# Attention and mixture-of-experts layer, one core: the first two chunks' work in another order, decay matrix and up-weight copy split

## The reference

```
weights = exp(tanh(((xn @ W + b) @ xn.T) * decay))      # decay[s,t] = 1/|s-t|, 0 on the diagonal
weights = weights * (1 - eye);  weights /= sum + 1e-7;  attn = weights @ xn
scores  = sigmoid(xn @ gate_w.T); top 2 of 8 experts by scores + expert_bias
h       = relu(up_e(score * xn))**2 in bf16; routed = sum over the two experts of down_e(h)   # hidden size 176
shared  = relu(xn @ shared_up.T)**2 @ shared_down.T
out     = x + attn + routed + shared
```

## Time and profile before

| | |
|---|---|
| median of 3 runs | 126.49 us |
| profiled execution, whole | 126.78 us |
| its span, first to last instruction | 125.0 us |
| PE busy | 113.0 us (90%) |
| DVE busy | 100.3 us (80%) |
| ACT busy | 90.5 us (72%) |
| POOL busy | 69.3 us (55%) |
| granted TensorE clock | 1.00 (2.4 GHz) throughout |

### The profile page before, as it was taken

The page is one execution under the profiler, slowest core; times in us unless marked ns, Lnnn a source line. Parts: engine busy times, 40 slices in busy tenths (PEclk is TensorE's granted clock), DMA queues, the critical chain, the costliest instruction groups (busy, mean ns, idle before and its releaser), DMA issues.

```text
span 125.0 us, 2786 instructions
## 1 busy us (share of the span) xinstructions
PE 113.0 (90%) x915; PEld 84.6 (68%) x915; DVE 100.3 (80%) x312; ACT 90.5 (72%) x133; POOL 69.3 (55%) x122
## 2 busy tenths in 40 slices
PE   2978874797999999999999999999999999999691
PEld 2964354375767877687958695878588767778491
DVE  5794794996888898898899889889888688988721
ACT  1215859697858977897969796988689768996730
POOL 4329827997499139943896369716981514141000
DMA  3999000699365993968394939487778656868952
GB/s 97 366 394 359 16 0 0 127 144 127 69 122 112 97 226 60 171 124 152 67 208 81 167 74 188 81 192 90 148 85 199 123 106 125 199 115 48 238 149 84
DMA packets 47821, 17.28 MB, mean 138 GB/s; under 512 B 44992, under 2 KB 45760, under 8 KB 47808
## 3 DMA queue, kind: packets, MB, share of 16 engines
q1 hardware_dynamic: 47232, 15.44, 63.3%
q10 hardware_dynamic: 576, 1.68, 3.8%
HBM read 3.84 MB, written 2.10 MB: 47 GB/s over the span
## 4 chain that ended last, share of the span: by engine, by line
PE 76%; POOL 8%; ACT 4%; DMA 4%; DVE 3%; issue 2%; POOLq 0%; DVEq 0%; ACTq 0%
PE out_ps L768 13%; PE h_ps L737 13%; PE side L714 10%; PE dots L697 9%; PE out_ps L756 5%; PE side L726 5%; PE out_ps L797 4%; PE small L689 4%; DMA hiddenT<-hidden 4%; PE out_ps L750 4%; PE small L674 3%; PE small L666 3%; POOL xn L242 3%; DVE gated L542 1%; PE small L683 1%
## 5 line engine op out<-in xcount | busy, mean ns | idle before, releaser
L542 DVE SCALAR_TENSOR_TENSOR gated<-h_ps,gates 128x1408 bf16<-128x1408 f32 x31 | 50.0, 1614 | 6.9 <-PE h_ps L737 5.9
L412 ACT ACTIVATE hidden<-gated 128x1408 bf16<-128x1408 bf16 x31 | 42.6, 1379 | 3.7 <-DVE gated L542 3.4
L768 PEld LDWEIGHTS out_ps<-downT,hiddenT 128*128 128x128 bf16 x341 | 21.6, 98 | 7.6 <-issue 3.4
L737 PE MATMUL h_ps<-upT,xnTb 128*128 128x512 bf16 (+1 forms) x96 | 24.4, 362 | 1.2 <-DVE gated L542 0.9
L768 PE MATMUL out_ps<-downT,hiddenT 128*128 128x128 bf16 x341 | 24.1, 219 | 1.2 <-DMA hiddenT<-hidden 1.2
L242 POOL TENSOR_SCALAR xn<-x_sb,meanvar,rstd 128x128 f32<-128x128 f32 x28 | 22.0, 796 | 0.7
L267 POOL TENSOR_SCALAR_AFFINE_SELECT probs<-probs 128x256 f32<-128x256 f32 x16 | 6.5, 408 | 23.5 <-ACT probs L378 23.5
L714 PE MATMUL side<-xn,probs 128*128 128x129 f32 x128 | 17.1, 276 | 0.8 <-POOL probs L267 0.8
L714 PEld LDWEIGHTS side<-xn,probs 128*128 128x128 f32 x128 | 15.9, 191 | 2.4 <-POOL probs L267 1.3
L697 PE MATMUL dots<-projT,xnT 128*128 128x256 f32 x60 | 16.0, 389 | 1.5 <-ACT projT L369 1.5
L737 PEld LDWEIGHTS h_ps<-upT,xnTb 128*128 128x128 bf16 x96 | 8.2, 98 | 8.3 <-DVE gated L542 2.0
(11 more groups left out here) (83 smaller groups left out, 162.3 us busy)
## 6 DMA issues: line engine op xcount, KB each, us to landing
x_sb<-in_x SPq DMA_DIRECT2D x7, 256.0 KB, 8.7
out_y<-final SPq DMA_DIRECT2D x7, 256.0 KB, 2.4
up_raw<-in_up ACTq DMA_DIRECT2D x1, 704.0 KB, 6.6
down_raw<-in_down ACTq DMA_DIRECT2D x1, 704.0 KB, 8.5
hiddenT<-hidden SPq DMA_TRANSPOSE x31, 3.7
out_y<-final SPq DMA_DIRECT2D x2, 128.0 KB, 1.7
late_sb<-in_late SPq DMA_DIRECT2D x1, 192.0 KB, 6.7
x_sb<-in_x ACTq DMA_DIRECT2D x1, 128.0 KB, 2.4
```

What stands on the lines that cost most here:

```text
L412: a.activation(hidden[:, t, :], gated[:, t, :], ACT.Square).then_inc(squared, 1)
L542: v.scalar_tensor_tensor(out=gated[:, t, :].rearrange("p (e h) -> p e h", e=E), in0=h_ps[:, 0:NH].rearrange("p (e h) -> p e h", e=E), scal ...
L737: last = t_.matmul(h_ps[:, at:to], xnTb[:, c % 4, t * P:(t + 1) * P], upT[:, at:to], start=True, stop=True)
L768: last = t_.matmul(out_at(t), hiddenT[:, c % 2, t, j, :], downT[:, j, :], start=(t == 0 and j == 0), stop=(t >= 2 and j == KT - 1), skip_g ...
```

## The change

All of it lies in the head and in the order of work of chunks 0 and 1.

- The distance matrix is built for 256 columns instead of 384. Of the decay matrix's four 128-column blocks the third, which was a DVE reciprocal of its own, is now the transpose of the second: PE turns it (`turn_decay`) and ACT copies it (`copy_decay`). `weigh(0, 0)` waits for that copy.
- `cast_up` is two instructions of 704 columns, one before `exp_logits(0)` and one after `take_proj(0)`; it was one of 1408 after `take_pair(0)`.
- DVE takes the statistics of chunk 0 in tile order 2, 3, 0, 1, with a semaphore for each half's load.
- Chunk 0's gates are made by one DVE instruction (`route_gates_first`) instead of two on POOL.
- `attend(0, 1)` writes a bank of its own (`attend_bank`), and chunk 1's projection goes to `side`.
- Passes 0 and 1 are written out by hand on all four engines; from pass 2 on the loops are as before, but `down_tile(0, 1)` now lies in pass 2. `rsqrt(0)` stays on POOL.

```diff
+            def route_gates_first():
+                dve.wait_ge(marks_set, 1)
+                v.scalar_tensor_tensor(out=gates[:, 0, :, :], in0=marked[:, :, 0:E], scalar=MARK, in1=scores[:, :, :],
+                                       op0=ALU.is_equal, op1=ALU.mult).then_inc(gates_ready, 1)
...
+            def turn_decay():
+                pe.wait_ge(inverse_made, 2)
+                t_.transpose(out_ps[:, 0:P], decay[:, P:2 * P], ident[:, :]).then_inc(decay_turned, 1)
...
+            def copy_decay():
+                act.wait_ge(decay_turned, 1)
+                a.activation(decay[:, 2 * P:3 * P], out_ps[:, 0:P], ACT.Copy).then_inc(decay_copied, 1)
...
             take_xT(0)
+            cast_up(0)
             exp_logits(0)
             act.wait_ge(early_loaded, 16)
             take_proj(0)
+            cast_up(1)
+            copy_decay()
+            take_pair(0)
             relu_rest(0)
-            take_pair(0)
-            cast_up()
...
+            normalize(1)
+            mask(0, 0)
+            square_rest(0)
+            cast_down()
+            rsqrt(2)
+            narrow(1)
+            normalize(2, 0, 2)
+            mask(0, 1)
+            normalize(2, 2, 4)
+            make_gates(1)
+            square_rest(1)
+            square_shared(0)
+            mask(1, 0)
+            add_x(0)
+            mask(1, 1)
```

More of the change, by code:

```diff
@@ L151, in proj_bank, with attend_bank @@
         def proj_bank(c):
-            return small if c else side
+            return small if c > 1 else side
+        def attend_bank(c, q):
+            return out_ps[:, CH:2 * CH] if c == 0 and q == 1 else side[:, :]
         LAST = NCH - 1
@@ L476, in norm_stats @@
             def norm_stats(c):
-                dve.wait_ge(x_loaded[c], 32 if c == 0 else 16)
-                for t in range(TILES):
+                order = (2, 3, 0, 1) if c == 0 else range(TILES)
+                if c > 0:
+                    dve.wait_ge(x_loaded[c], 16)
+                for t in order:
+                    if c == 0 and t % 2 == 0:
+                        dve.wait_ge(x_first[t // 2], 16)
                     v.bn_stats(stats[:, t, :], x_sb[:, c, t, :]).then_inc(stats_step, 1)
@@ L522, in route_mark @@
                 dve.wait_ge(pair_set, c + 1)
-                wait(dve, hot_step, c)
+                wait(dve, hot_step, c - 1)
                 for t in range(TILES):
@@ L592, in _ @@
             norm_stats(0)
-            decay_inverse(1, 2)
             normalize_first()
             norm_stats(1)
-            decay_inverse(2, 3)
-            for k in range(0, NCH):
-                f, c, o, g = k, k - 1, k - 2, k + 1
[L599 to L605, removed]
+            decay_inverse(1, 2)
@@ new lines, in _ @@
+            route_one(0)
+            route_scores(0)
+            route_bias(0)
+            route_top(0)
+            weigh(0, 0)
+            route_mark(0)
+            route_gates_first()
+            gate(0, 0)
+            weigh(0, 1)
+            norm_stats(2)
+            gate(0, 1)
+            route_one(1)
+            route_scores(1)
+            route_bias(1)
+            route_top(1)
+            gate(0, 2)
+            route_mark(1)
+            weigh(1, 0)
+            attend_sums(0, 0)
@@ L606, in _ @@
+            attend_norm(0, 0)
+            attend_sums(0, 1)
+            gate(0, 3)
+            attend_norm(0, 1)
+            attend(0)
+            weigh(1, 1)
+            for k in range(2, NCH):
+                f, c, o, g = k, k - 1, k - 2, k + 1
+                gate(c, 0)
+                attend_sums(c, 0)
+                attend_norm(c, 0)
+                if g < NCH:
                     norm_stats(g)
[L607 to L610, removed]
+                gate(c, 1)
+                finish(o, 0)
@@ L803, in _ @@
             transpose_exp(0)
+            turn_decay()
             dots(0, 0)
+            up_tile(0, 0)
             dots(0, 1)
-            up_tile(0, 0)
-            shared_main(0)
-            up_tile(0, 1)
-            transpose_x(1)
-            for k in range(1, NCH):
+            transpose_x(1)
+            rest(1)
+            up_tile(0, 1)
+            project(1)
+            transpose_exp(1)
+            shared_main(0)
+            up_tile(0, 2)
+            attend(0, 0)
+            dots(1, 0)
+            attend(0, 1)
+            up_tile(0, 3)
+            dots(1, 1)
+            transpose_x(2)
+            down_tile(0, 0)
+            for k in range(2, NCH):
                 f, c, o = k, k - 1, k - 2
-                back = o >= 0
-                if c >= 1:
-                    up_tile(c, 0)
+                up_tile(c, 0)
+                if k == 2:
+                    down_tile(0, 1)
                 attend(c, 0)
                 rest(f)
[L817 to L823, removed]
+                shared_down_rest(o)
+                up_tile(c, 1)
+                shared_down_main(o)
+                down_tile(o, 2)
                 transpose_exp(f)
@@ L827, in _ @@
                 project(f)
-                if c >= 1:
-                    shared_main(c)
-                if back:
-                    down_tile(o, 3)
+                shared_main(c)
+                down_tile(o, 3)
                 dots(f, 0)
```

171 lines of the change are left out of this document (92 added, 79 removed).

## The result

The changed kernel takes 124.47 us (median of 4 runs, 123.95 to 124.78), the kernel before in the same session 126.31 us. The ratio is 0.985, 95% interval 0.980 to 0.990. The interval leaves out 1, so it is faster, by 1.84 us, about half of the 3.7 that were forecast. The profiled execution took 124.2 us with a span of 122.3 us, 2.7 us less than before.

The account below looks back on a forecast made before the run. PE is gapless from 30 to 109 us, so starting that stretch (`attend(1, 0)`) 3.7 us earlier carries to the end: 126.78 - 3.7 - 0.29 = 122.8 us. Own range 122.3 to 123.5; 8 in 10: 122.0 to 124.2.

Parts of the forecast that it names:

- Step 1: Start of the chain: one iota less moves the head that hangs on PE up 0.20 us, bounds 0 and 0.20.
- Step 2: Up weights copied in halves on ACT, 0.85 us each; the first fits idle time before the exponential, cost at most 0.1.
- Step 3: Decay block by PE transpose and ACT copy, done by 12.5 us, when `weigh(0, 0)` starts; bad end 12.7.
- Step 4: Chunk 0's gates on DVE take 0.35 us with their wait; `gate(0, 0)` starts at 14.06, gain so far 0.55.
- Step 5: DVE runs without gaps for 9.33 us from `gate(0, 0)` to `gate(0, 3)`, which starts at 23.39; gain 2.67 us.
- Step 6: From `gate(0, 3)` to `attend(1, 0)`, which starts at 26.3 us instead of 29.99; gain 3.7 us.
- third check: DMA transpose of tile 1, before `down_tile(0, 1)`: issued at 21.8 us, there at 25.4, needed at 25.65.
- The late transpose: Rival before `down_tile(0, 1)`: landing takes 4.9 us, there at 26.7, PE stands still 1.05; time 123.9 us, chance 0.11.
- DVE and POOL block each other: Rival: a shared SBUF port lock delays gates on DVE and `normalize_first`, 1.1 us in all; time 123.9, chance 0.04.
- The steady passes lose their step: Rival in the loop: PE waits once a chunk, paid 6 times; at 0.8 us each 127.6 us, chance 0.03.
- No more than the first gate: Rival: something keeps `attend(1, 0)` late, so only 0.55 us of gain remains; time 125.9 us, chance 0.03.
- More gain: Rival: small waits put between the links are mostly hidden; gain 4.2 to 4.6 us, time 122.1, chance 0.09.

Follow-up runs that it names:

- e7: The order of e3, with the up weights copied in one instruction after `take_pair(0)`, as before the change: 123.68 us, ratio 0.974.
- e0: The changed kernel again without any edit, for a second trace and its spread: 124.65 us, ratio 0.985.
- e2: The changed kernel, with SP issuing the transpose of tile (0, 2) only after that of (0, 1) has landed: 123.24 us, ratio 0.976.
- e8: The changed kernel with 6 tiny matmuls added on PE ahead of `rest(1)`: 123.16 us, ratio 0.970.
- e3: The changed kernel with `down_tile(0, 1)` moved behind `attend(1, 0)` and `rest(2)` on PE: 123.56 us, ratio 0.975.
- e4: The changed kernel with 32 tiny matmuls added in PE's idle time, 64 instructions with their weight loads: 122.38 us, ratio 0.964.
- e6: The order of e3, with chunk 0's gates again on POOL, between chunk 1's third and fourth normalising instructions: 124.96 us, ratio 0.985.

## Why the prediction came out as it did

**Links 1 to 5 held.** Step 1: `take_proj(0)` at 10.53 and `route_one(0)` at 10.69, forecast 10.58 and 10.74. Step 2: the halves took 0.79 and 0.78 us, estimate 0.85, and the first waited 0.16 for its load (landing 7.0, not the 6.6 of the earlier trace rows); the exponential behind it still started on time (9.43), but the split is worth little (e7). Step 3: `weigh(0, 0)` at 12.54, forecast 12.5; the ACT copy of the block took 0.27. Step 4: the gates took DVE 0.19 us and 0.30 with what lies around them, forecast 0.35; `gate(0, 0)` at 14.13, forecast 14.06. Step 5: `gate(0, 3)` at 23.45, forecast 23.39, with DVE idle 0.26 us before it for PE:

```profile
22.96 0.17 DVE L609 RECIPROCAL rownorm<-rowsum 128x2 f32<-128x2 f32 x1
23.04 0.14 DVE L605 TENSOR_SCALAR rowsum<-out_ps 128x2 f32<-128x2 f32 x1
23.45 1.63 DVE L583 SCALAR_TENSOR_TENSOR gated<-h_ps,gates 128x1408 bf16<-128x1408 f32 x1 [0.26 <-PE h_ps L806]
```

**Step 6 failed, in the third check.** `up_tile(1, 0)` started at 25.22 (forecast 25.06), POOL's `mask(1, 0)` ran from 25.42 to 25.83 (forecast 25.2 to 25.7), in time for 26.3. The check that failed reads "with 3.6 us to landing it is there at 25.4, needed at 25.65". The issue at 21.8 was right (21.7), the landing was not: 5.3 us, there at 27.05. The term that failed is the 3.6 us to landing. Of the shortfall of 1.42 us at `attend(1, 0)` (27.72 against 26.30) 1.12 is this wait, 0.16 the late `up_tile`, 0.16 that it was over 0.75 us after its start and not 0.59.

**The late transpose as rival had the right place and nearly the right price, and the wrong chance.** It was priced at a wait of 1.05 us and 123.9 us of time; measured 1.12 and 124.47. That the wait fits so well is in part luck: the transpose landed 0.35 us later than the rival had it, and PE was ready 0.32 later. I gave it 0.11 by counting: one of 12 transposes took 4.9 us, so I treated that row as a rare accident. In the whole trace of before, 6 of 31 took 4.2 us or more. It was no accident either. In the kernel before, the fetch at 27.64 fell into tile (0, 2)'s transpose issued at 26.4, which had room. A landing that is late in one row was late for a reason, and the reason moves with the program. The change pulls tiles (0, 1) and (0, 2) under the fetch together, and (0, 1), which has no room, was hit in both profiled executions.

**The end of the forecast had a second hole.** It took the tail as fixed: "126.78 - 3.7 - 0.29". The tail's transpose was under a fetch before (4.7) and still is (4.35 to 5.0), so the tail can give or take some tenths between executions: in e0 the head is 2.4 us earlier than before and the span only 2.2. Where the head's wait is gone the sum is right: e2 and e8 have spans 3.7 below before, and medians of 123.24 and 123.16 us, 3.4 and 3.7 below the kernel before beside them. Where the tail's fetch is gone too, 122.38.

**The other rivals.** *DVE and POOL block each other*: not seen. `normalize_first` took 1.17 us beside POOL's two selects, 1.12 before, and the gates on DVE took 0.19 inside a POOL normalisation of 1.58:

```profile
6.39 1.17 DVE L523 TENSOR_SCALAR xn<-x_sb,meanvar,rstd 128x128 f32<-128x128 f32 x4 [1.48 <-POOL rstd L241]
6.42 0.56 POOL L259 TENSOR_SCALAR_AFFINE_SELECT decay<-decay 128x128 f32<-128x128 f32 x2
...
12.44 1.58 POOL L246 TENSOR_SCALAR xn<-x_sb,meanvar,rstd 128x128 f32<-128x128 f32 x2
```

(These are two instructions of 0.79, and the gates, from 13.83 to 14.02, lie inside the second.) By the rule of the Trainium skill weighed in the prediction ("SBUF — State Buffer", section "Who interferes with whom") the gates, with two inputs in SBUF, would have stood behind it until 14.02; the measurement decides against the rule for these forms. *The steady passes lose their step*: PE is busy 79.00 of 79.00 us. *No more than the first gate*: `gate(0, 3)` and `mask(1, 0)` were in time. *More gain*: no, step 5 came out at 9.32 us, forecast 9.33.

## What to carry to other kernels

Where a step's slack is smaller than the spread of a transfer's landing, the largest row of that transfer is the forecast until its cause is known; look at what else was in the queues when it was slow. A long unrolled program has its own traffic: when an engine stands for a DMA that is late in one place and not in others, look for an instruction packet there. Three things helped here: independent work between issue and use (e3), which holds wherever the fetch falls; holding back the second transpose where it has time (e2); and moving the fetch (e4), which any later edit can undo.

When two theories are named as rivals, allow for both being needed. Here one experiment took away the second transpose (e2), another the fetch (e4), and each alone made the landing normal.

## What the runs showed of the hardware

- In 200 of 372 DMA transposes (128 x 1408, bf16) no instruction packet was near, and they landed in 3.5 to 3.8 us. Every one of the 63 that took 4.2 to 5.5 us had one near: one packet of 16 KB (0.9 to 1.8 us long) or of 8 KB.
- Where a transpose's packets kept coming behind the start of a fetch, one landed in 4.35 us or more, 20 times out of 20. In the changed kernel no packet started from 25.5 to 26 us, and 241 did in the us of the fetch where e4, without one, has 823. Why one packet holds up the others is not shown.
- A transpose whose own packets were all through landed 1.3 to 1.4 us late when a fetch came and the packets of a second one stood behind it (0, 1: 1.89 us from last packet to landing in the changed kernel, 0.61 in e2, 0.50 in e4).
- Adding TensorE instructions moves the fetches, but not in proportion: 12 moved the first one by 4.1 us, 64 by 7.5. That queue 8 is TensorE's is inferred from this and from the count of 262 instructions to a packet. Time moves it too: in e7, with no instruction added, it came at 27.28 and not at 25.12 as in e3.
- After PE had been busy 0.69 of 2 us, with a pause of 1.19, the granted clock averaged 0.69 for 4 us (e6).
